# Attention scores by seven block products instead of eight, in a gated cross-attention and feed-forward block

## The chip, the cores and the metric

The kernel runs on one core of one Trainium2 chip. The metric is the device time of one execution in microseconds (us): 608.14 for the kernel before, the median of 3 runs (607.65 to 608.43). The engines are TensorE (PE; its weight loads are listed apart as PEld), VectorE (DVE), ScalarE (ACT), GpSimd (POOL) and SyncE (SP), which here issues every DMA. Each engine works through its own instructions in the order in which they are written; semaphores are all that ties them together.

## The reference

```
x   = x + tanh(g_xattn) * attn(layernorm(x), ctx, ctx, wq, wk, wv, wo)      # x: 4 x 512 x 512, ctx: 4 x 512 x 512
        q = xn wq^T;  k = [ctx, xn wk^T];  v = [ctx, xn wv^T]               # 512 queries, 1024 keys in each batch
        out = softmax(q k^T / sqrt(512)) v wo^T
x   = x + tanh(g_ffn) * ffn(layernorm(x))
        hidden = relu((xn sign(up)^T) * up_scale)                           # 2048 wide
        ffn = (hidden sign(down)^T) * down_scale * output_scale
```

All in float32. The four batches are independent.

## The kernel before, in words

**Precision.** TensorE is used at float32r. Each float32 operand is split in two, HI (ACT copies it to float32r) and LO (DVE or POOL subtracts HI from the original), and a product of split operands is three matmuls (`PASSES`, L14): HI·HI, HI·LO, LO·HI. A matmul here is always 128 x 128 weights against 512 columns.

**One batch of attention** on TensorE, in order: 96 matmuls of scores (4 tiles of 128 queries by two sides, "ctx" and "new", by 4 chunks by 3 passes), with the probabilities of each tile turned by 8 transposes through the two `turn` banks; 48 matmuls for V (`v_terms`, four jobs of 12); 96 for probabilities times V (`attn_terms`, four groups e = 0 to 3 of 24, each 12 "new" and 12 "old"); 48 for the output projection (`out_piece`); and 96 for the next batch's K and Q (eight jobs of 12). A job writes one PSUM bank; ACT takes HI from the bank, DVE then takes LO from the same bank, and only then is the bank free (`proj_out`, L754 and L994). Groups e = 0, 2 share bank 0 of `proj`, groups e = 1, 3 share bank 1.

**Scores and softmax** (L478, L1009, L758). A tile's 1024 scores stay in PSUM; DVE takes the maximum from there, ACT the exponential from there into `probs`, which has room for two tiles.

**Layernorm of the next batch.** DVE takes statistics of the next batch's rows (L1021, L1026, L1047), POOL the inverse deviation (L367). SP stores these facts to DRAM (`row_facts`, L306, 4 KB), waits for the store, and loads them back along the free axis for all partitions (`all_facts`, L309, 512 KB). DVE then normalises `turned_x`, the already transposed input (`norm_turned`, L1032 and L1035), ACT takes HI (L853), DVE takes LO (L1040), and K and Q of the next batch can start. In ACT's program L853 stands between the copies of groups e = 0 and e = 1. In DVE's program the statistics stand among the softmax of the batch, and `norm_turned` after V's last split.

**Context.** `raw_ctx` is loaded twice in a batch, transposed (for the scores) and plain (for the values). ACT splits off HI (L748), POOL takes LO (L382).

**Last batch.** Beside its attention the first rows of the feed-forward input are normalised, turned (`turn_two`) and copied out by ACT (L784), and the signs of the weights are taken by ACT (`take_signs`, L769 to L779) from one buffer `raw_w`, which SP refills (512 KB) after each (`load_signs`, L259). In ACT's program the first sign steps stand one behind each exponential. The feed-forward part (from about 374 us on) uses the same seven-product form that the change brings to the scores, and is not touched.

**Start.** ACT and POOL split the four weight matrices while TensorE makes K and Q of batch 0; ACT's program mixes these splits (`weight_high`, L744) with the copies of K and Q.

## Time and profile before

| | |
|---|---|
| time, median of 3 runs | 608.14 us (607.65 to 608.43) |
| the profiled execution's own time | 608.41 us |
| its span, first to last instruction | 606.6 us |
| TensorE busy | 598.5 us, 99% of the span |
| chain of work that ended last | 95% TensorE |
| granted TensorE clock, mean | 1.000 |
| a batch, from one batch's first score matmul to the next's | 90.7 us |

The profile is one execution. "Busy" of TensorE counts pipelined matmuls, so a row's mean time of one matmul (about 390 ns) is longer than the distance from one to the next; the distance is read from the starts of consecutive groups. Idle time of an engine stands in brackets, with what ended it. The program's lines (L454) are those of the kernel before.

### The profile page before, as it was taken

What the parts mean: (1) busy time and instruction counts of PE and PEld (TensorE: products, weight loads), DVE (VectorE), ACT (ScalarE), POOL (GpSimd) and SP (SyncE); (2) the same over time, 40 slices, a digit from 0 to 9 for tenths busy, and PEclk for the clock granted to TensorE, in tenths of its full rate; (3) what the DMA queues carried; (4) which work ended last, traced back from release to release, by engine and by line L of the source; (5) the groups of instructions that cost most, each with busy time, mean ns of one, the idle gap of its engine ahead of it and who ended that gap; (6) DMA issues with size and microseconds to landing.
All of it is one profiled execution on the core that took longest, in us unless ns stands there. A gap on an engine that the chain in (4) does not pass through costs nothing.

```text
span 606.6 us, 6935 instructions
## 1 busy us (share of the span) xinstructions
PE 598.5 (99%) x2786; PEld 496.8 (82%) x2786; DVE 298.5 (49%) x439; ACT 245.1 (40%) x366; POOL 126.5 (21%) x116
## 2 busy tenths in 40 slices
PE   8999999999999999999999999999999999999997
PEld 7888888888888888888888888888887878888885
DVE  4335532225632225632226658665548844766664
ACT  3723321213321214321125655564658545645531
POOL 5760303000303000303000305224132003242002
PEclk9999999999999999999999999999999999999999
DMA  8751303000303000503012212112121212241011
GB/s 299 273 171 38 106 1 110 29 0 1 104 1 131 8 0 1 239 4 104 1 36 70 89 52 78 62 35 71 35 70 35 83 56 70 70 133 42 1 70 69
DMA packets 20096, 43.20 MB, mean 71 GB/s; under 512 B 4832, under 2 KB 4832, under 8 KB 19680
## 3 DMA queue, kind: packets, MB, share of 16 engines
q1 hardware_dynamic: 20064, 42.76, 20.6%
q8 instruction: 22, 0.36, 0.3%
q14 instruction: 10, 0.08, 0.0%
HBM read 36.45 MB, written 6.30 MB: 70 GB/s over the span
## 4 chain that ended last, share of the span: by engine, by line
PE 95%; DVE 2%; ACT 1%; DMA 1%; SPq 0%; issue 0%; ACTq 0%
PE proj L454 33%; PE score L454 22%; PE score L532 19%; PE turn L517 12%; PE proj L517 5%; PE turn L446 2%; PE score L669 2%; DMA rows<-in_x 1%; PE proj L500 1%; PE turn L500 1%; DVE four_x L991 0%; ACT four_x L748 0%; DVE rows L1335 0%; DVE scaled L1332 0%; DVE neg_max L1011 0%; ACT probs L760 0%
## 5 line engine op out<-in xcount | busy, mean ns | idle before, releaser
L532 PE MATMUL score<-down_signs,hid_split 128*128 128x512 f32 x512 | 133.8, 390 | 0.6 <-DVE normed L1245 0.5
L532 PEld LDWEIGHTS score<-down_signs,hid_split 128*128 128x128 f32 x512 | 95.8, 188 | 21.7 <-DVE hid_split L1212 0.9
L756 ACT ACTIVATE four_x<-proj 128x512 fp32r<-128x512 f32 x60 | 35.8, 599 | 163.3 <-PE proj L454 163.3
L454 PE MATMUL score<-four_x 128*128 128x512 f32 x384 | 89.9, 391 | 0.0
L454 PE MATMUL proj<-probsT,four_x 128*128 128x512 f32 x384 | 88.4, 390 | 0.0
L454 PEld LDWEIGHTS proj<-probsT,four_x 128*128 128x128 f32 x384 | 71.9, 188 | 14.8
L454 PEld LDWEIGHTS score<-four_x 128*128 128x128 f32 x384 | 71.5, 188 | 14.5
L454 PE MATMUL proj<-four_x,weights 128*128 128x512 f32 x336 | 76.8, 389 | 0.0
L454 PEld LDWEIGHTS proj<-four_x,weights 128*128 128x128 f32 x336 | 63.0, 188 | 13.0
L997 DVE TENSOR_TENSOR four_x<-proj,four_x 128x512 fp32r<-128x512 f32 x44 | 30.3, 691 | 87.9 <-ACT four_x L756 87.9
L382 POOL TENSOR_TENSOR four_x<-raw_ctx,four_x 128x2048 fp32r<-128x2048 f32 x8 | 36.9, 4610 | 116.5 <-ACT four_x L748 116.5
L1212 DVE TENSOR_TENSOR hid_split<-hid,hid_split 128x512 fp32r<-128x512 f32 x64 | 44.0, 690 | 15.8 <-ACT hid_split L910 15.5
L517 PE MATMUL turn<-ops_b,up_ops 128*128 128x512 f32 x192 | 51.8, 391 | 0.0
L910 ACT ACTIVATE hid_split<-hid 128x512 fp32r<-128x512 f32 x64 | 39.9, 630 | 21.7 <-PE score L532 18.9
L760 ACT ACTIVATE probs<-score,neg_max 128x1024 f32<-128x1024 f32 x16 | 17.9, 1117 | 71.8 <-DVE neg_max L1011 71.8
L454 PE MATMUL proj<-weights,four_x 128*128 128x512 f32 x192 | 46.0, 394 | 0.3 <-DVE four_x L997 0.3
L454 PE MATMUL score<-weights,four_x 128*128 128x512 f32 x192 | 45.3, 389 | 0.0
L901 ACT ACTIVATE hid<-hid,hid_gain 128x512 f32<-128x512 f32 x48 | 34.8, 724 | 22.3 <-DVE hid L1227 11.0
L415 POOL TENSOR_TENSOR up_ops<-up_ops 128x256 fp32r<-128x256 f32 x16 | 13.3, 831 | 145.0 <-ACT up_ops L779 145.0
L454 PEld LDWEIGHTS score<-weights,four_x 128*128 128x128 f32 x192 | 36.0, 188 | 7.5
L517 PEld LDWEIGHTS turn<-ops_b,up_ops 128*128 128x128 f32 x192 | 35.7, 188 | 7.2
L454 PEld LDWEIGHTS proj<-weights,four_x 128*128 128x128 f32 x192 | 35.4, 188 | 7.5 <-DVE four_x L997 0.5
(102 smaller groups left out, 645.9 us busy)
## 6 DMA issues: line engine op xcount, KB each, us to landing
raw_w<-in_ffn_w SPq DMA_DIRECT2D x24, 512.0 KB, 3.3
raw_ctx<-in_ctx_turned SPq DMA_DIRECT2D x4, 1024.0 KB, 8.1
raw_ctx<-in_ctx SPq DMA_DIRECT2D x4, 1024.0 KB, 5.4
result<-rows SPq DMA_DIRECT2D x16, 256.0 KB, 2.1
rows<-in_x SPq DMA_DIRECT2D x3, 1024.0 KB, 5.5
turned_x<-in_x_turned SPq DMA_DIRECT2D x3, 1024.0 KB, 7.8
rows_away<-rows SPq DMA_DIRECT2D x1, 2048.0 KB, 10.4
rows<-rows_away SPq DMA_DIRECT2D x1, 2048.0 KB, 7.8
```

Of the source, the lines that this page charges most:

```text
L382: pool.tensor_tensor(ctx_side[:, LO], raw_ctx[:, :, :], ctx_side[:, HI].bitcast(F32), ALU.subtract).then_inc(ctx_ready, 1)
L415: pool.tensor_tensor(a[:, S3], a[:, A11].bitcast(F32), a[:, A21].bitcast(F32), ALU.subtract).then_inc(left_ready, 1)
L446: last = pe.transpose(bank[:, k * P:(k + 1) * P], tile, ident[:, :])
L454: last = pe.matmul(bank, lhs(l), rhs(r), start=start and i == 0, stop=stop and i == 2)
L517: last = pe.matmul(bank, up_ops[:, g % 2, left, c * P:(c + 1) * P], right(i)[:, s, c, :], start=start and c == 0 and s == HI, stop=stop an ...
L532: last = pe.matmul(wide(r), hid_split[:, n % HR, s, r * P:(r + 1) * P], down_signs[:, chunk_of(q), :], start=(q == 0 and s == HI), stop=(q ...
L756: act.activation(dst, proj_bank(n), ACT.Copy, scale=scale).then_inc(proj_hi, 1)
L760: act.activation(probs[:, t % 2, :], score[t % 2][:, :, :].rearrange("p a n -> p (a n)"), ACT.Exp, bias=neg_max[:, t:t + 1], accum_out=row ...
L901: act.activation(dst, src, ACT.Relu, scale=hid_gain[:, j:j + 1]).then_inc(relu_done, 1)
L910: act.activation(hid_split[:, n % HR, HI, :], src, ACT.Copy).then_inc(hid_hi, 1)
L997: dve.tensor_tensor(dst(LO), proj_bank(n), dst(HI).bitcast(F32), ALU.subtract).then_inc(proj_lo, 1)
L1212: dve.tensor_tensor(hid_split[:, n % HR, LO, :], src, hid_split[:, n % HR, HI, :].bitcast(F32), ALU.subtract).then_inc(hid_ready, 1)
```

## The change

The scores of a batch are taken as one product of a left matrix (Q, 512 x 512) and a right matrix (the keys, 512 x 1024), each cut in two by two blocks: A11, A12, A21, A22 on the left and B11, B21 (context) and B12, B22 (new keys) on the right. Seven block products of sums take the place of eight: S3·T3, S2·T2, S1·T1 and so on. Each is 2 tiles by 2 chunks by 3 passes, 12 matmuls, 84 in a batch. To form them, K and Q go from PSUM into SBUF unsplit (`raw_new`, `raw_q`), DVE makes the sums T1 to T4 and S1 to S4, ACT and DVE split each; after the products DVE adds PSUM banks and partial sums into `probs`, which now holds all four tiles in SBUF. Maximum and exponential work on `probs`.

The probabilities are turned in eight blocks of 4 transposes, one in the middle of each V job and one behind it. Before group e = 0 TensorE waits once for the splits of all four V jobs. `raw_ctx`, `turned_x` and `normed` are one memory. The statistics of the next batch, `norm_turned` and the sign steps stand at other places. Order of TensorE's products: A11, S3, A12, S2, S1, A22, S4.

```diff
-        probs = at("probs", 192, [P, 2, KEYS])
-        raw_ctx = at("raw_ctx", 200, [P, RT, DIM])
+        probs = at("probs", 192, [P, RT, KEYS])
+        first_normed = at("first_normed", 200, [P, RT, DIM])
+        raw_ctx = at("raw_ctx", 208, [P, RT, DIM])
         normed = at("normed", 208, [P, RT, DIM])
+        turned_x = at("turned_x", 208, [P, DC, ROWS])
+        raw_q = at("raw_q", 120, [P, DC, ROWS])
+        raw_new = at("raw_new", 152, [P, DC, ROWS])
+        raw_t = at("raw_t", 176, [P, KC, ROWS])
+        s3_op = at("s3_op", 216, [P, 2, 2, 2 * P], F32R)
...
+        SCORE_ORDER = (A11, S3, A12, S2, S1, A22, S4)
+        SCORE_RIGHT = {A11: B11, S3: T3, A12: B21, S2: T2, S1: T1, A22: T4, S4: B22}
+        TILE_ORDER = (2, 3, 0, 1)
+        OLD, NEW = 0, 1
+        TURN_ORDER = ((2, NEW), (2, OLD), (3, NEW), (3, OLD), (0, NEW), (1, NEW), (0, OLD), (1, OLD))
...
+            def context_rows(b):
+                sp.wait_ge(ctx_ready, turned_split(b) + 1)
+                sp.wait_ge(t_sums, nth(T_SUMS, b, T4))
+                sp.dma_start(raw_ctx[:, :, :], ctx_v[b]).then_inc(ctx_in, 16)
...
+                sp.wait_ge(ctx_ready, values_split(b - 1) + 1)
                 sp.dma_start(turned_x[:, :, :], x_turned_v[b]).then_inc(turned_x_in, 16)
                 sp.wait_ge(rstd_done, b)
                 sp.wait_ge(means_out, b)
                 sp.dma_start(row_facts[b - 1].rearrange("s r p -> p s r"), mean_rstd[:, :, :],
                              allow_slow_non_contiguous=True).then_inc(facts_stored, 16)
...
+                sp.wait_ge(scored, product_scored(b - 1, S3, 1))
                 sp.dma_start(all_facts[:, :, :], row_facts[b - 1:b].rearrange("a s r p -> a s (r p)").broadcast_to(
...
+            for b in range(BATCH):
+                context_rows(b)
+                if b + 1 < BATCH:
+                    next_rows(b + 1)
+                    sp.wait_ge(next_lo, b + 1)
+                    sp.dma_start(raw_ctx[:, :, :], ctx_turned_v[b + 1]).then_inc(ctx_in, 16)
...
             for i in range(DC):
                 weight_low(W_V, i)
             for b in range(BATCH):
+                context_low(values_split(b))
                 inverse_std(b + 1)
...
+            def score_product(b, i, t):
+                for c in range(2):
+                    for k, (l, r) in enumerate(PASSES):
+                        last = pe.matmul(score_bank(i, t), q_left(i, l)[:, c, t * P:(t + 1) * P],
+                                         key_right(SCORE_RIGHT[i], r)[:, c, :],
+                                         start=i in (A11, S3, S2) and c == 0 and k == 0, stop=c == 1 and k == 2,
+                                         skip_group_check=True)
...
+            def scores(b):
+                pe.wait_ge(ctx_ready, turned_split(b) + 1)
+                pe.wait_ge(s_ready, nth(S_LO, b, A11))
+                for t in range(2):
+                    pe.wait_ge(raw_kq, kq_out(b, DC + 2 + t))
+                    score_product(b, A11, t)
+                pe.wait_ge(t_ready, nth(T_LO, b, T3))
+                pe.wait_ge(s_ready, nth(S_LO, b, S3))
+                pe.wait_ge(attended, RT * b)
...
+                for r in range(RT):
+                    if r < 2:
+                        pe.wait_ge(score_c11, 2 * b + r + 1)
+                    else:
+                        pe.wait_ge(proj_lo, values_out(b, r - 2))
+                    for i, (lhs, rhs) in enumerate(v_terms(r)):
+                        last = product(proj_bank(proj0(b) + r), lhs, rhs, i == 0, i == DC - 1)
+                        if i == 1:
+                            turn_probs(b, 2 * r)
+                    last.then_inc(proj_done, 1)
+                    turn_probs(b, 2 * r + 1)
...
+                scores(b)
+                v_jobs(b)
+                pe.wait_ge(proj_lo, values_out(b, RT - 1))
+                pe.wait_ge(turn_lo, turn0(b) + 6)
                 for e in range(DC):
                     new, old = attn_terms(e)
-                    pe.wait_ge(proj_lo, n + 4 + e - 1)
+                    if e >= 1:
+                        pe.wait_ge(proj_lo, values_out(b, DC + e - 2))
                     for i, (lhs, rhs) in enumerate(new):
-                        if e == 0:
-                            pe.wait_ge(proj_lo, n + i + 1)
                         last = product(proj[:, e % 2, :], lhs, rhs, i == 0, False)
+                    if last_batch and e < 2:
+                        turn_two(RT * e)
                     if e == 0:
+                        pe.wait_ge(turn_lo, turn0(b) + 2 * RT)
...
+                n = e if b == 0 else proj0(b - 1) + 8 + e
+                act.wait_ge(proj_done, n + 1)
+                act.activation(raw_new[:, e, :], proj_bank(n), ACT.Copy).then_inc(raw_kq, 1)
...
+            def keys_and_queries(b, e):
+                if e < DC:
+                    key_out(b, e)
+                else:
+                    query_out(b, e - DC)
+                if e == 1:
+                    t_high(b, T1)
+                if e == DC:
+                    t_high(b, T3)
+                    t_high(b, T2)
+                if e == DC + 1:
+                    s_high(b, A11)
+                    s_high(b, S3)
+                    t_high(b, T4)
+                if e == DC + 2:
+                    t_high(b, B22)
...
                 context_high(values_split(b))
+                exponentials(b, 2)
...
+                proj_out(m + 3, new_side[:, HI, 3, :])
+                probs_out(b, 7)
                 if last_batch:
+                    for n in range(4):
+                        take_signs(n)
+                    two_rows_out(0)
                     take_signs(4)
...
+            def s_sum(b, i):
+                    dve.wait_ge(t_sums, nth(T_SUMS, b, T3))
+                    dve.wait_ge(raw_kq, kq_out(b, DC + 1))
+                elif i == S2:
+                    dve.wait_ge(raw_kq, kq_out(b, DC + 3))
+                    dve.wait_ge(s_ready, nth(S_LO, b, S3))
+                elif i == S4:
+                    dve.wait_ge(s_sums, nth(S_SUMS, b, S2))
+                dve.tensor_tensor(dst, one, two, op).then_inc(s_sums, 1)
...
+                bank = score[0 if k in (AT_P17, AT_C21) else 1][:, t, :]
+                if k in (AT_P17, AT_P16):
+                    plus = probs[:, t, 512:1024]
+                    dve.wait_ge(score_p1, 2 * b + t + 1)
+                else:
+                    plus = dst
+                    dve.wait_ge(score_sums, score_sum(b, {AT_C22: AT_P17, AT_C21: AT_P16, AT_C12: AT_P16}[k], t))
+                dve.wait_ge(scored, product_scored(b, last_product, t))
+                dve.tensor_tensor(dst, bank, plus, ALU.add).then_inc(score_sums, 1)
...
+            def keys(b):
+                t_sum(b, T1)
+                t_sum(b, T3)
+                t_sum(b, T2)
+                t_sum(b, T4)
+                t_low(b, T3)
...
+                proj_out(b, 3, chunk(new_side, 3))
+                probs_out(b, 7)
                 dve.wait_ge(exp_done, RT * b + RT)
...
+                    dve.wait_ge(ctx_ready, values_split(b) + 1)
+                    norm_rows(b + 1, 0)
+                    norm_stats(RT)
+                    norm_moments(BATCH + 1)
+                    proj_out(b, 4, chunk(qT, 0))
                     for f in range(RT, 2 * RT):
...
                 else:
-                    for e in range(DC):
-                        proj_out(m + 4 + e, chunk(qT, e))
-                        if e == 1:
-                            next_rows_low(b + 1)
+                    dve.wait_ge(x_in[b + 1], 16)
+                    norm_stats(next_tile0)
+                    norm_moments(b + 1)
+                    means(b + 1)
+                    proj_out(b, 4, chunk(qT, 0))
+                    norm_turned(b + 1)
+                    proj_out(b, 5, chunk(qT, 1))
+                    next_rows_low(b + 1)
+                    proj_out(b, 6, chunk(qT, 2))
+                    proj_out(b, 7, chunk(qT, 3))
+                if b + 2 == BATCH:
+                    norm_stats(0)
+                    norm_moments(BATCH)
+                keys(b + 1)
```

DVE, batch 0, from the first turned probabilities to the split of the next rows. L1021 to L1047 are the statistics of the next batch's rows, L1032 and L1035 its normalisation (`norm_turned`), L997 splits of V jobs and, behind L1129, of groups e. Before:

```order
L991 TENSOR_TENSOR probsT<-turn,probsT 128x4x128 x2
L1021 BN_STATS stats<-rows 128x6 x4
L1011 TENSOR_REDUCE neg_max<-score 128x1
L1026 BN_AGGR mean_var<-stats 128x2 x4
L1047 COPY mean_rstd<-mean_var 128x4
L991 TENSOR_TENSOR probsT<-turn,probsT 128x4x128 x2
L1011 TENSOR_REDUCE neg_max<-score 128x1
L991 TENSOR_TENSOR probsT<-turn,probsT 128x4x128 x2
L997 TENSOR_TENSOR four_x<-proj,four_x 128x512 x2
L991 TENSOR_TENSOR probsT<-turn,probsT 128x4x128 x2
L997 TENSOR_TENSOR four_x<-proj,four_x 128x512 x2
L1032 TENSOR_TENSOR turned_x<-turned_x,all_facts 128x2048
```

The same place after the change (L1179 is the split of V jobs and of groups e, L1174 of turned probabilities, L1288 to L1314 the statistics, L1299 and L1302 the normalisation, L1307 the LO part of the next rows):

```order
L1179 TENSOR_TENSOR four_x<-proj,four_x 128x512
L1174 TENSOR_TENSOR probsT<-turn,probsT 128x4x128
L1388 RECIPROCAL row_inv<-row_sum 128x4
L1392 TENSOR_SCALAR row_gain<-row_inv,gates 128x4
L1288 BN_STATS stats<-rows 128x6 x4
L1293 BN_AGGR mean_var<-stats 128x2 x4
L1314 COPY mean_rstd<-mean_var 128x4
L1179 TENSOR_TENSOR four_x<-proj,four_x 128x512
L1299 TENSOR_TENSOR turned_x<-turned_x,all_facts 128x2048
L1302 TENSOR_TENSOR turned_x<-turned_x,all_facts 128x2048
L1179 TENSOR_TENSOR four_x<-proj,four_x 128x512
L1307 TENSOR_TENSOR four_x<-turned_x,four_x 128x2048
```

The statistics moved from among the softmax, ahead of all V splits, to behind the last split of V and of the probabilities; the normalisation stands behind the split of group 0 and ahead of that of group 1.

ACT in the last batch, behind the last turned probabilities (L873) of that batch. L964 are sign steps, L969 copies of turned feed-forward rows, L877 the copy of group e = 0. After the change:

```order
L873 ACTIVATE probsT<-turn 128x4x128
L964 ACTIVATE down_signs<-raw_w 128x1024 x4
L969 ACTIVATE raw_x_72<-turn 128x4x128 x2
L964 ACTIVATE down_signs<-raw_w 128x1024
L877 ACTIVATE four_x<-proj 128x512
L969 ACTIVATE raw_x_72<-turn 128x4x128 x2
```

Before, the last of the sign steps that stand apart, with the same copies (L779 sign steps, L784 turned rows, L756 copies of V jobs 2 and 3):

```order
L779 ACTIVATE down_signs<-raw_w 128x1024
L756 ACTIVATE four_x<-proj 128x512
L784 ACTIVATE raw_x_67<-turn 128x4x128 x2
L756 ACTIVATE four_x<-proj 128x512
L784 ACTIVATE raw_x_67<-turn 128x4x128 x2
L779 ACTIVATE down_signs<-raw_w 128x1024
```

Four sign steps now follow one another without other work between them, and the copies that free the `turn` banks come behind them.

## Rows read from the trace of the kernel before

**Rows 1.** The page's busy table: engine, busy us (share of the span), instructions.
```profile
PE 598.5 (99%) x2786; PEld 496.8 (82%) x2786; DVE 298.5 (49%) x439; ACT 245.1 (40%) x366; POOL 126.5 (21%) x116
```

**Rows 2.** What TensorE waited for: us in total, times, longest.
```profile
PE score L676 <- DVE ones L1181: 1.2, 1, 1.2
...
PE proj L454 <- DVE four_x L997: 0.3, 1, 0.3
```

**Rows 3.** TensorE in order of time, batch 1: start us, us, instructions.
```profile
124.95 11.05 PE L454 MATMUL score<-four_x 128*128 128x512 f32 x48
135.84 1.03 PE L446 MATMUL turn<-ident,probs 128*128 128x128 f32 x8
136.63 5.71 PE L454 MATMUL score<-four_x 128*128 128x512 f32 x24
```

**Rows 4.** Timeline, a job's end, its two splits, and the next batch's statistics.
```profile
125.15 0.60 ACT L756 ACTIVATE four_x<-proj 128x512 fp32r<-128x512 f32 x1 [2.12 <-PE proj L454]
125.78 0.69 DVE L1000 SCALAR_TENSOR_TENSOR four_x<-proj,four_x 128x512 fp32r<-128x512 f32 x1 [2.03 <-ACT four_x L756]
...
143.73 0.37 DVE L1026 BATCH_NORM_AGGREGATE mean_var<-stats 128x2 f32<-128x6 f32 x4
...
145.50 0.37 SPq L306 DMA_DIRECT2D row_facts<-mean_rstd  x1
...
156.42 0.34 SPq L309 DMA_DIRECT2D all_facts<-row_facts  x1
...
162.67 2.28 DVE L1032 TENSOR_TENSOR turned_x<-turned_x,all_facts 128x2048 f32<-128x2048 f32 x1
164.98 2.29 DVE L1035 TENSOR_TENSOR turned_x<-turned_x,all_facts 128x2048 f32<-128x2048 f32 x1
...
167.36 1.91 ACT L853 ACTIVATE four_x<-turned_x 128x2048 fp32r<-128x2048 f32 x1
```

**Rows 5.** SP's two facts DMAs in the other batches, from its timeline.
```profile
54.83 0.37 SPq L306 DMA_DIRECT2D row_facts<-mean_rstd  x1
66.39 0.34 SPq L309 DMA_DIRECT2D all_facts<-row_facts  x1
...
236.18 0.37 SPq L306 DMA_DIRECT2D row_facts<-mean_rstd  x1
245.31 0.34 SPq L309 DMA_DIRECT2D all_facts<-row_facts  x1
```

**Rows 6.** The facts' load (line L309): issue to landing.
```profile
DMA to landing us min/median/max: 3.4/3.6/5.9
```

**Rows 7.** ACT and TensorE at the start.
```profile
20.68 0.60 ACT L756 ACTIVATE four_x<-score 128x512 fp32r<-128x512 f32 x1 [0.84 <-PE score L669]
21.18 1.14 ACT L744 ACTIVATE weights<-rows 128x512 fp32r<-128x512 f32 x2
...
23.36 11.07 PE L454 MATMUL proj<-four_x,weights 128*128 128x512 f32 x48
```

**Rows 8.** Groups of 1024 columns, and of the whole context: busy us, mean ns.
```profile
L1079 DVE TENSOR_TENSOR normed<-raw_x 128x1024 f32<-128x1024 f32 x2 | 2.4, 1217 | 0.0
...
L800 ACT ACTIVATE ops_a<-raw_x 128x1024 fp32r<-128x1024 f32 x8 | 8.3, 1055 | 0.0
...
L748 ACT ACTIVATE four_x<-raw_ctx 128x2048 fp32r<-128x2048 f32 x8 | 15.3, 1917 | 0.0
```

**Rows 9.** Last batch: two sign steps on ACT, and DVE around them.
```profile
345.46 0.17 DVE L1127 RECIPROCAL row_inv<-row_sum 128x4 f32<-128x4 f32 x1
...
345.80 1.91 DVE L1059 TENSOR_SCALAR normed<-rows,mean_var,mean_rstd 128x512 f32<-128x512 f32 x4
347.63 2.46 DVE L1021 BATCH_NORM_STATS2 stats<-rows 128x6 f32<-128x512 f32 x4
...
372.06 1.05 ACT L779 ACTIVATE down_signs<-raw_w 128x1024 fp32r<-128x1024 f32 x1
...
376.44 1.06 ACT L779 ACTIVATE up_ops<-raw_w 128x1024 fp32r<-128x1024 f32 x1 [0.78 <-DMA raw_w<-in_ffn_w]
```

**Rows 10.** TensorE, last batch: first score matmul, and the output projection's first.
```profile
306.31 11.05 PE L454 MATMUL score<-four_x 128*128 128x512 f32 x48
...
368.52 5.60 PE L454 MATMUL score<-weights,four_x 128*128 128x512 f32 x24
```

**Rows 11.** TensorE's first matmuls of 256 columns.
```profile
1.19 5.09 PE L676 MATMUL score<-ones 128*128 128x256 bf16 x23 [1.19 <-DVE ones L1181]
6.13 0.84 PE L446 MATMUL turn<-ident,normed 128*128 128x128 f32 x4
...
7.57 1.04 PE L676 MATMUL score<-ones 128*128 128x256 bf16 x8
```

More of the change, by code:

```diff
@@ L74, in sem @@
             return stack.enter_context(nc.semaphore(name))
+        A11, A12, A21, A22, S1, S2, S3, S4 = range(8)
+        B11, B21, B22, T1, T3, T2, T4 = range(7)
         KB = 1024
@@ L104, in gated_block @@
         hid1_slots = at("hid1", 112, [P, HC, ROWS])
-        A11, A12, A21, A22, S1, S2, S3, S4 = range(8)
         up_ops = at("up_ops", 144, [P, 2, 8, 2 * P], F32R)
@@ L491, in turn_probs, with score_bank @@
-            def turn_probs(b, t):
-                pe.wait_ge(exp_done, RT * b + t + 1)
-                for half in range(2):
-                    turn_job(turn0(b) + 2 * t + half, cols(probs[:, t % 2, half * 512:(half + 1) * 512]))
+            def score_bank(i, t):
+                if i in (A11, A12):
+                    return proj[:, t, :]
+                return score[0 if i in (S3, A22) else 1][:, t, :]
+            def score_product(b, i, t):
[5 more added lines that the diff above has]
+                                         skip_group_check=True)
+                last.then_inc(scored, 1)
@@ new lines, in first_products_out @@
+            def first_products_out(b):
+                s_high(b, A12)
+                s_high(b, S2)
+                for t in range(2):
+                    act.wait_ge(scored, product_scored(b, A11, t))
+                    act.activation(probs[:, t, 512:1024], proj[:, t, :], ACT.Copy).then_inc(score_p1, 1)
+                s_high(b, S4)
+                s_high(b, S1)
+                for t in range(2):
+                    act.wait_ge(scored, product_scored(b, A12, t))
+                    act.activation(probs[:, t, 0:512], proj[:, t, :], ACT.Copy).then_inc(score_c11, 1)
```

389 lines of the change are left out of this document (235 added, 154 removed).

## The prediction

> **What bounds the kernel now.** I read the busy table first: TensorE works 99% of the span, DVE 49%, ACT 40% [rows 1]. Then what TensorE waited for: nothing above 1.2 us, and in the attention 0.3 us [rows 2]. Then TensorE in order of time, where groups follow one another without a gap [rows 3]: 48 score matmuls from 124.95 to 135.84 are 0.227 us each; a block of 8 transposes takes 0.79 (135.84 to 136.63). So each matmul that goes is worth 0.227 us, and each wait that TensorE gets is paid in full. The other engines have idle time, but in fixed orders, so what counts is where their instructions stand.
>
> **Product count.** 96 score matmuls of a batch become 84: 12 x 0.227 = 2.7 us, over four batches **-10.9 us**. Eight blocks of 4 transposes for four of 8: at 0.79 for 8, no change.
>
> **Do the sums keep up?** Take t = 0 as the end of the last Q job. A job's end is followed by the copy after 0.20, the DVE step starts 0.63 after that and takes 0.69, 1.5 in all [rows 4]; DVE steps of 1024 columns take 1.22, ACT's 1.05 [rows 8]. T1 to T4 follow K's jobs, all summed by -6.3; the last raw Q copy ends at 0.8. A11 can start at 0 (tile 0 needs Q chunk 2 only) and S3 at 2.7 (its split ends near -2.5). A12 is due at 5.4, its split ends near 2.9; S2 due at 8.2, split near 3.6; S1 due at 10.9, split near 5.7; tile 1 of S1 at 12.2 needs the sum of S2's second bank, at 11.8, the narrowest place. The maximum of tile 2 ends near 17, that of tile 3 near 20; the first turned block is due at 20.4, the third at 24.0, when the first one's split ends near 23.3. So the score stage of a running batch costs nothing. If one link slips, a few tenths in each batch.
>
> **Start.** Here it does not keep up. ACT's program puts the new copies between weight splits. K's second copy ends at 21.3 [rows 7]. Then: T1 on DVE 1.2, its copy 1.05, weight pair 1.15, K2 0.6, context 1.9, K3 0.6, weight pair 1.15, Q0 0.6, which ends at 29.3 with ACT's overlaps. TensorE's Q jobs start at 23.36 [rows 7], and the third, due at 28.8, waits for that copy: 0.5. Two T copies, a weight pair and Q1's copy end at 32.9: fourth job 0.9. Then A11, S3, T4, a weight pair, Q2 end at 36.8 (1.2 lost at tile 0 of A11), B22, the last pair and Q3 at 39.5 (1.3 lost at tile 1). Sum **+4.0**, between 2 (T1 faster, overlaps larger) and 6.
>
> **V's last split.** Groups e took V's four splits one by one before. Now TensorE waits for all four before e = 0. The last V job's split is ready 1.5 after its end, and only one block of 4 transposes, 0.4, lies in between. 1.1 x 4 = **+4.5**. Between 1 and 1.5 each.
>
> **The facts of the next rows.** This is the main term. Before, DVE took the statistics among the softmax, so that the trip of the facts to DRAM and back lay beside V. Now they stand behind the last split. Let v be the end of the last V job. Split of V at v+1.5, of the last probabilities +2.2, reciprocal and gain 0.34 (+2.5) and four statistics 2.46 (+5.0) [rows 9], aggregates to the issue of the store 143.73 to 145.50, 1.8 (+6.8) [rows 4]. Store's issue to load's issue: 10.9 there, 11.6 and 9.1 in the other batches [rows 4, 5], mean 10.5 (+17.3). Load 3.6 (+20.9) [rows 6]. Two normalisation steps 162.67 to 167.27, 4.6 (+25.5); L853 on ACT 1.9 (+27.4) [rows 4]. Queued behind it on ACT is the copy of group e = 1, and behind the normalisation on DVE its split: 0.6 and 0.7 (+28.7). That split frees bank 1 of `proj`, for which group e = 3 waits. TensorE has groups 0, 1, 2 as cover: 1.5 + 72 x 0.227 = +17.8. So it waits 10.9 us in batches 0, 1 and 2: **+32.7**. With the shortest trip (9.1 + 3.4) 9.3 each, with the longest (11.6 + 5.9) 14.3. Behind that nothing else is late: K and Q need the next rows' LO part (2.3 us of DVE more), and TensorE has e = 3 and the output projection, 72 x 0.227 = 16 us, before them. POOL's inverse deviation and the load of `turned_x` stand behind the context's split, which ends some 18 us ahead of v.
> The Trainium skill (DMA: Bandwidth & Descriptors, Anatomy of one DMA) gives about 2.0 us of fixed cost for a DMA of its GpSimd path. Taken for the 4 KB store the wait would be about 8.5 shorter in each batch, an estimate by that page; the trace shows 9.1 to 11.6 three times, so I go by the trace.
>
> **Signs in the last batch.** ACT takes four sign steps in a row. `raw_w` is one buffer, so each waits for its refill: from one start to the next 372.06 to 376.44, 4.4 us [rows 9]. After the last turned probabilities at v+1.4: first sign until +2.5, the fourth until +15.6, and only then the copy of the first turned feed-forward row, +16.2, for which the third block of turns waits. TensorE is there at 1.5 + 2.7 + 0.8 + 2.7 = +7.8: 8.4 us. Then the fifth sign (+20.0), the copy and split of e = 0 (+21.3), and behind it on DVE the next normalised row (0.5, +21.8), due at +19.8: 2.0. Together 10.4. From the batch's first score to the output projection it took 62.2 before [rows 10], of which 240 x 0.227 + 8 x 0.79 = 60.8 is work: 1.4 of old waits go. **+9.0**, between 5 and 13.
>
> **TensorE's clock.** TensorE's first 23 matmuls of 256 columns, after it had done nothing, took 4.9 us, 0.215 each, and 8 like them at 7.57 took 1.04 with the last one's tail [rows 11]. 256 columns in 0.215 us is the lower level, 1.2 GHz, though the view gives 1.000 as the mean granted clock. An idle stretch of 10.9 us may do the same again: half of 4.9 is 2.5 us lost behind each of the three waits. In the last batch most of it falls into the second wait, 0.5. **+8.0**, between 0 (no fall) and 12.
> The Trainium skill (TensorE: Matmul & The Clock Gate, The HAM clock gate) says that the clock is halved after an idle stretch and comes back after sustained work. By that the drop comes at each of the long waits; the rows of before agree for the start, and hold no long wait later that could test it.
>
> **Sum**, on the profiled execution's own 608.4: -10.9 + 4.0 + 4.5 + 32.7 + 9.0 + 8.0 = +47.3, so 655.7. The median of the runs is 0.3 below that execution. I say **656 us**.
>
> **Rivals.**
> The clock stays up through waits of 10 us. For it: in all rows the granted clock reads 1.000. Against it: the start's matmuls. 656 - 8 = 648 us.
> The facts return early, since in the new order no other transfer is in flight. For it: the range 9.1 to 11.6 within one run. Against it: at 145.50 to 156.42 nothing else was in flight either, and it took 10.9. With a trip of 6 instead of 14.1 the wait is 2.8 each and the clock has no reason to fall: 656 - 24.3 - 7.5 = 624 us.
> More waits than I counted, at the joints of the score stage (0.4 of slack at S1) or with a longer slow stretch of the clock behind each wait: 1 us in each batch and 4.9 for the 2.5 of each fall give 656 + 4 + 7 = 667 us.
> Faster than before: the cover holds everywhere and only the product count is left. This is one mechanism, the facts' trip: it decides from where the split of e = 1 is ready at v+17.8, which needs a trip of 3.2 us instead of 14.1. Then, if also the sign steps found cover, 608.4 - 10.9 + 4.0 + 4.5 = 606; with no wait at the start or behind V either 597.5. Against it stand the three measured trips.
>
> **How the numbers follow.** The forecast (640 to 661 on its own) 0.55, the steady clock 0.17, the early facts 0.10, more waits 0.13, faster 0.05. The range goes from 642, below the steady clock's case with the shortest trip in part, to 666, near the third rival: what is left out is the early facts, the faster case and the outer part of the others, about 0.2. What a measurement can tell from no change here is about 0.2%, 1.2 us: faster by more 0.04, within 0.01, slower 0.95.
>
> **What would show it.** In the profile after: 336 score matmuls; TensorE idle about 11 us before group e = 3 in batches 0, 1, 2, put down to the split of e = 1 (DVE) with the facts' load ahead of it; about 1 us before e = 0 in each batch; 8 and 2 us among the turned rows of the last batch, ended by ACT or DVE behind the sign steps; about 4 us over the last Q jobs and A11 of batch 0; and matmuls at twice the distance, with a granted clock below 1, behind each long wait. The period of a batch goes from 90.7 to 90.7 - 2.7 + 1.1 + 10.9 + 2.5 = 102.5 us. A period of 88 to 90 would prove the main term wrong, as would facts that are stored before the last split of V.

## The result, and the profile after

The changed kernel takes 663.73 us (median, 663.20 to 664.76) against 608.08 for the kernel before on the same chip: a ratio of 1.092, 95% interval 1.090 to 1.094. The profiled execution has a span of 662.5 us where before it was 606.6, so 55.9 us are to be found. In each fence below the lines are those of the kernel named ahead of it.

The changed kernel's page, its busy table, and what TensorE waited for (us in total, times, longest), to be read against [rows 1, 2]:

```profile
PE 602.3 (91%) x2738; PEld 494.3 (75%) x2738; DVE 382.2 (58%) x527; ACT 290.0 (44%) x426; POOL 132.7 (20%) x116
```

```profile
PE proj L527 <- DVE four_x L1179: 35.2, 7, 11.2
PE turn L625 <- ACT raw_x L969: 7.7, 1, 7.7
PE proj L527 <- ACT raw_q L888: 5.8, 2, 5.6
PE proj L560 <- ACT raw_q L888: 1.9, 1, 1.9
```

There are 48 matmuls fewer, as the product count says, and yet TensorE is busy 3.8 us longer: it is slower somewhere. And there are now four kinds of wait where there was hardly any.

**Start.** TensorE in order of time, changed kernel, from Q's four jobs (the first two on one line) over the first score product (A11, at 44.99) to the second (S3, at 49.61):

```profile
23.96 5.63 PE L527 MATMUL proj<-four_x,weights 128*128 128x512 f32 x24
29.79 3.01 PE L527 MATMUL proj<-four_x,weights 128*128 128x512 f32 x12 [0.19 <-ACT raw_q L888]
38.37 4.75 PE L527 MATMUL proj<-four_x,weights 128*128 128x512 f32 x12 [5.58 <-ACT raw_q L888]
44.99 4.78 PE L560 MATMUL proj<-four_x 128*128 128x512 f32 x12 [1.87 <-ACT raw_q L888]
49.61 2.89 PE L560 MATMUL score<-probsT,s_op 128*128 128x512 f32 x12
```

A product of 12 matmuls takes 2.72 from its start to the next one's, so a score stage at full speed that reaches S3 at 49.61 would have begun at 46.89. Before, it began at 34.27. The start costs 12.6 us. In it are the two waits of 5.6 and 1.9, the two groups that took 4.8 us where 12 matmuls take 2.9, and a first Q job 0.6 later than in [rows 7]. The slow groups are the clock's: it read 0.72 around the first of them and 0.66 around the second (45.00 to 50.00). The first stretch (start and end us, length, busy us of PE, PEld, DVE, ACT, POOL, the granted clock, DMA share, GB/s):

```profile
38.40:45.00 6.60, 4.73 (x13) 3.48 (x13) 6.50 (x6) 3.74 (x7) 3.84 (x3) 0.72 0.00 0
```

DVE and POOL in the same stretch:

```profile
21.99 1.23 DVE L1200 TENSOR_TENSOR raw_t<-raw_new,raw_ctx 128x1024 f32<-128x1024 f32 x1 [3.93 <-ACT raw_new L883]
28.15 5.25 DVE L1200 TENSOR_TENSOR raw_t<-raw_new 128x1024 f32<-128x1024 f32 x1 [4.93 <-ACT raw_new L883]
33.32 2.29 DVE L1200 TENSOR_TENSOR raw_t<-raw_new,raw_t 128x1024 f32<-128x1024 f32 x1
35.65 2.18 DVE L1200 TENSOR_TENSOR raw_t<-raw_ctx,raw_t 128x1024 f32<-128x1024 f32 x1
```

```profile
27.71 4.60 POOL L455 TENSOR_TENSOR four_x<-raw_ctx,four_x 128x2048 fp32r<-128x2048 f32 x1 [0.26 <-ACT four_x L869]
32.27 4.46 POOL L450 TENSOR_TENSOR weights<-probs,weights 128x512 fp32r<-128x512 f32 x2
```

The four lines of DVE are the same instruction at the same size: T1, T3, T2, T4. T1, with nothing of POOL beside it, takes 1.23. T3 begins 0.44 behind POOL's context split and ends 1.1 behind that split's end (28.15 + 5.25 = 33.40, 27.71 + 4.60 = 32.31), as if it did nothing until POOL was through and then took its own time; experiments 3 and 4 test this. Each of POOL's two W_O splits behind it takes 2.23, where 1.3 is usual.

**A batch.** SP, DVE and ACT of the changed kernel, from the statistics behind batch 0's last split of probabilities to the split for which group e = 3 waits (the answer to [rows 4]):

```profile
83.16 2.47 DVE L1288 BATCH_NORM_STATS2 stats<-rows 128x6 f32<-128x512 f32 x4
...
102.34 2.29 DVE L1299 TENSOR_TENSOR turned_x<-turned_x,all_facts 128x2048 f32<-128x2048 f32 x1 [12.88 <-DMA all_facts<-row_facts]
104.66 2.29 DVE L1302 TENSOR_TENSOR turned_x<-turned_x,all_facts 128x2048 f32<-128x2048 f32 x1
109.41 0.69 DVE L1179 TENSOR_TENSOR four_x<-proj,four_x 128x512 fp32r<-128x512 f32 x1 [2.46 <-ACT four_x L877]
```

```profile
87.45 0.37 SPq L379 DMA_DIRECT2D row_facts<-mean_rstd  x1
98.49 0.34 SPq L384 DMA_DIRECT2D all_facts<-row_facts  x1
```

```profile
106.99 1.91 ACT L1044 ACTIVATE four_x<-turned_x 128x2048 fp32r<-128x2048 f32 x1 [18.25 <-DVE turned_x L1302]
```

TensorE beside it, and a stretch with the granted clock (columns as above):

```profile
82.37 16.61 PE L527 MATMUL proj<-probsT,four_x 128*128 128x512 f32 x72 [0.98 <-DVE four_x L1179]
110.16 7.45 PE L527 MATMUL proj<-probsT,four_x 128*128 128x512 f32 x24 [11.18 <-DVE four_x L1179]
117.44 0.84 PE L527 MATMUL score<-weights,four_x 128*128 128x512 f32 x3
```

```profile
110.00:114.00 4.00, 3.84 (x9) 3.05 (x10) 2.90 (x3) 0.00 (x0) 0.00 (x0) 0.52 0.05 18
```

The chain is the one of the forecast: statistics behind the last split, a store that needs 11.0 to the load's issue, two normalisation steps, ACT's copy, the late split of e = 1. The wait ahead of e = 0 is 1.0. Behind the wait of 11.2 the granted clock is 0.52 for 4 us, the lower of TensorE's two levels, and e = 3 takes 7.28 from its start to the next group's, not 5.44. In batches 1 and 2 the wait is 10.4 and 9.8, the group 7.58 and 8.08. From one batch's first score product to the next's it takes 102.0 and 101.9 (150.08, 252.09, 353.98), and 103.2 from the 46.89 worked out above to 150.08. Before, it was 90.7.

**Last batch.** TensorE of the changed kernel around its wait:

```profile
392.40 2.98 PE L527 MATMUL proj<-probsT,four_x 128*128 128x512 f32 x12
403.05 1.97 PE L625 MATMUL turn<-ident,normed 128*128 128x128 f32 x8 [7.67 <-ACT raw_x L969]
404.67 4.27 PE L527 MATMUL proj<-probsT,four_x 128*128 128x512 f32 x12
```

ACT ahead of it, changed kernel (the copy for which TensorE waits is the third line):

```profile
397.12 1.06 ACT L964 ACTIVATE down_signs<-raw_w 128x1024 fp32r<-128x1024 f32 x1 [3.34 <-DMA raw_w<-in_ffn_w]
401.45 1.06 ACT L964 ACTIVATE down_signs<-raw_w 128x1024 fp32r<-128x1024 f32 x1 [3.27 <-DMA raw_w<-in_ffn_w]
402.41 1.06 ACT L969 ACTIVATE raw_x<-turn 128x512 f32<-128x512 f32 x2
```

Sign steps 4.3 to 4.4 apart, as in [rows 9]. From the first score product (353.98) to the output projection (424.32) it is 70.3 us, 8.1 more than [rows 10]. The feed-forward network behind it takes 238 us in both kernels.

The 55.9 us are thus 12.6 at the start, 35.0 in the three periods, 8.1 in the last batch, and 0.2 for rounding and the feed-forward part.

### The profile page after: what moved, and what is told of

It is laid out like the page before. It is cut to its first block, busy times and chain, and to the rows that moved or that the text cites. A ratio compares the mean times of both kernels' runs of the same rounds, so it can differ in the third digit from the quotient of the medians.

```text
span 662.5 us, 7100 instructions
## 1 busy us (share of the span) xinstructions
PE 602.3 (91%) x2738; PEld 494.3 (75%) x2738; DVE 382.2 (58%) x527; ACT 290.0 (44%) x426; POOL 132.7 (20%) x116
## 4 chain that ended last, share of the span: by engine, by line
PE 68%; DMA 9%; issue 8%; DVE 8%; ACT 5%; POOL 2%; SPq 0%; POOLq 0%; DVEq 0%; ACTq 0%
PE proj L527 19%; PE score L657 17%; PE turn L642 11%; PE score L527 7%; DMA row_facts<-mean_rstd 4%; PE proj L642 4%; PE score L560 4%; PE proj L560 2%; DMA all_facts<-row_facts 2%; DVE raw_t L1200 2%; DMA raw_w<-in_ffn_w 1%; POOL four_x L455 1%; PE score L788 1%; DVE turned_x L1299 1%; DVE turned_x L1302 1%
## 5 line engine op out<-in xcount | busy, mean ns | idle before, releaser
L527 PE MATMUL proj<-probsT,four_x 128*128 128x512 f32 x384 | 97.7, 416 | 35.2 <-DVE four_x L1179 35.2
L527 PEld LDWEIGHTS proj<-probsT,four_x 128*128 128x128 f32 x384 | 76.8, 203 | 53.9 <-DVE four_x L1179 37.5
L527 PE MATMUL proj<-four_x,weights 128*128 128x512 f32 x336 | 79.2, 396 | 5.8 <-ACT raw_q L888 5.8
L1179 DVE TENSOR_TENSOR four_x<-proj,four_x 128x512 fp32r<-128x512 f32 x32 | 22.0, 689 | 54.4 <-ACT four_x L877 54.4
L527 PE MATMUL proj<-weights,four_x 128*128 128x512 f32 x192 | 51.9, 405 | 0.0
L877 ACT ACTIVATE four_x<-proj 128x512 fp32r<-128x512 f32 x32 | 18.7, 593 | 55.9 <-PE proj L527 55.9
L527 PEld LDWEIGHTS proj<-weights,four_x 128*128 128x128 f32 x192 | 34.0, 189 | 5.9
L642 PE MATMUL proj<-ops_a,up_ops 128*128 128x512 f32 x128 | 34.6, 392 | 0.0
L1243 DVE TENSOR_TENSOR probs<-score,probs 128x512 f32<-128x512 f32 x40 | 27.5, 689 | 11.6 <-PE score L560 11.2
L642 PE MATMUL turn<-ops_a,up_ops 128*128 128x512 f32 x128 | 34.2, 389 | 0.0
```

Of the source, the lines that this page charges most:

```text
L527: last = pe.matmul(bank, lhs(l), rhs(r), start=start and i == 0, stop=stop and i == 2)
L642: last = pe.matmul(bank, up_ops[:, g % 2, left, c * P:(c + 1) * P], right(i)[:, s, c, :], start=start and c == 0 and s == HI, stop=stop an ...
L877: act.activation(dst, proj_bank(n), ACT.Copy).then_inc(proj_hi, 1)
L1179: dve.tensor_tensor(dst(LO), proj_bank(proj0(b) + i), dst(HI).bitcast(F32), ALU.subtract).then_inc(proj_lo, 1)
L1243: dve.tensor_tensor(dst, bank, plus, ALU.add).then_inc(score_sums, 1)
```

## The experiments

All runs are compared with the kernel before on their own chip; its median was 607.96 to 608.59. Names are those of the changed kernel's program.

**1. Statistics two batches ahead.**

```
 # DVE, batch(b), between V's splits and proj_out(b, 4)
-    dve.wait_ge(x_in[b + 1], 16)
-    norm_stats(next_tile0); norm_moments(b + 1); means(b + 1)
 # DVE, behind attend(b, r), ahead of keys(b + 1)
+    dve.wait_ge(x_in[b + 2], 16)
+    norm_stats(RT * (b + 2)); norm_moments(b + 2); means(b + 2)      # b = 0 and 1
 # and those of batch 1 between T1 and T3 of batch 0
```

> The changed kernel with one edit: the statistics of the rows two batches on are taken on DVE behind the output projection's last additions (those of batch 1 between T1 and T3 of batch 0), so that the facts are stored from about 17 us after a batch's first score product on instead of 7 us behind the last V job. Theory (the facts' trip is late, and its idle stretch drops TensorE's clock): the waits before group e = 3 in batches 0 to 2 (11.5, 10.7 and 10.1 us by the starts of the groups) and the slow matmuls behind them (1.8, 2.1, 2.6 us) go: 663.7 - 32.3 - 6.6 = 625 us. Rival (the split of e = 1 is late for another reason in ACT's or DVE's order): the waits stay, 663 us. Rival (the clock falls for another reason): the waits go and e = 3 still takes 7.3 to 8.1 us instead of 5.4: 631 us.

Measured: 625.08 us (624.75 to 626.16), ratio 1.027 (1.025 to 1.030): 38.65 us less. TensorE, batch 0 of this kernel: all four groups e in one stretch.

```profile
81.59 22.05 PE L527 MATMUL proj<-probsT,four_x 128*128 128x512 f32 x96 [0.98 <-DVE four_x L1179]
```

The three waits ahead of e = 3 (11.18, 10.39 and 9.78, by the starts 32.2 in all) and the slow groups behind them (6.6) are 38.8. The main term and the clock's term behind its waits have their cause shown.

**2. The last batch's sign steps spread among the score copies and probabilities.**

```
 # ACT, last batch
     context_high(values_split(b))
+    take_signs(0); take_signs(1)
     ...
     probs_out(b, 3)
+    take_signs(2)
     ...
     probs_out(b, 5)
+    take_signs(3)
     ...
-    for n in range(4): take_signs(n)
     two_rows_out(0)
```

> The changed kernel with one edit: in the last batch the first four sign steps stand apart in ACT's program, two ahead of the first exponential, one each behind the turned blocks 3 and 5. Theory (a row of sign steps waits for the refills of one buffer, and the copy that frees the turn bank stands behind it): the wait of 7.7 us before the third pair of turned rows goes, and the 1 to 2 us behind it: 663.7 - 10 = 654 us. Rival (the turned rows wait for something else, normalised rows or POOL): the wait stays, 663 us.

Measured: 653.00 us (652.00 to 656.94), ratio 1.074 (1.070 to 1.078): 10.7 us less. TensorE of this kernel goes through the same place without a wait:

```profile
391.56 2.99 PE L527 MATMUL proj<-probsT,four_x 128*128 128x512 f32 x12
394.39 1.04 PE L625 MATMUL turn<-ident,normed 128*128 128x128 f32 x8
```

**3 and 4. What stretched the T sums?** One kernel holds POOL's context split and W_O splits back until T4 is summed, the other holds back only a load of 1 MB that runs in the same stretch.

```
 # 3: POOL
+    pool.wait_ge(t_sums, nth(T_SUMS, 0, T4))
     context_low(turned_split(0))
 # 4: SP
+    sp.wait_ge(t_sums, nth(T_SUMS, 0, T4))
     sp.dma_start(rows[:, 2 * RT:3 * RT, :], x_v[2]).then_inc(x_in[2], 16)
```

> The changed kernel with one edit: at the start POOL waits for T4's sum before it splits the context, so that POOL does nothing while DVE takes T3, T2 and T4. Theory A (DVE steps with two SBUF operands and POOL's two-operand steps shut each other out): T3's sum takes 1.2 us instead of 5.25, T2's and T4's 1.2 instead of 2.3 and 2.2; Q's second raw copy comes about 5 us earlier, the fourth Q job no longer waits 5.6 us, the clock stays up there; POOL's context split then runs against T3's split and the S sums, which gives a part back: 663.7 - 3 to - 7, about 659 us. Theory B (the load of 1 MB of rows that lands in those 5 us slows DVE): T3 stays at 5.25, and the time does not fall.

> The changed kernel with one edit: at the start the load of batch 2's rows (1 MB, issued at 27.5 us) waits for T4's sum, so that no transfer lands while DVE takes T3, T2 and T4; POOL works as in the changed kernel. Theory A (POOL and DVE shut each other out): T3's sum stays at 5.2 us and the time is the same, 663.7. Theory B (the transfer slows DVE): T3's sum takes 1.2 us and the time falls by about 8, to 656.

Measured: 664.64 us (662.82 to 666.86) and 664.67 us (663.52 to 664.91), both ratio 1.092. With the load held back T3 still took 5.26: the transfer is not the cause. With POOL held back, DVE of that kernel, T3, T2, T4, the split of T3, and then S3's sum, which takes 0.68 by itself:

```profile
26.95 1.23 DVE L1201 TENSOR_TENSOR raw_t<-raw_new 128x1024 f32<-128x1024 f32 x1 [4.94 <-ACT raw_new L884]
28.09 1.22 DVE L1201 TENSOR_TENSOR raw_t<-raw_new,raw_t 128x1024 f32<-128x1024 f32 x1
29.35 1.23 DVE L1201 TENSOR_TENSOR raw_t<-raw_ctx,raw_t 128x1024 f32<-128x1024 f32 x1
30.49 1.22 DVE L1206 TENSOR_TENSOR probsT<-raw_t,probsT 128x1024 fp32r<-128x1024 f32 x1
32.03 4.66 DVE L1223 TENSOR_TENSOR raw_new<-raw_q 128x512 f32<-128x512 f32 x1 [0.32 <-ACT raw_q L889]
```

```profile
30.65 5.49 POOL L455 TENSOR_TENSOR four_x<-raw_ctx,four_x 128x2048 fp32r<-128x2048 f32 x1 [4.40 <-DVE raw_t L1201]
```

The mechanism is shown in both directions: each engine's step gets longer when it comes second. POOL's split, which came while DVE worked on the split of T3, takes 5.49 instead of 4.6; DVE's sum, which came while POOL worked, ends 0.55 behind POOL's end. But the time did not fall: the fourth Q job now waits 0.5 instead of 5.6, while A11 waits 4.9 and A12 2.6. I had expected 659. The stall was moved onto the next steps of DVE, since POOL's work still lay among them.

This kernel's cost is one of pairing. In the kernel before, POOL does the same context and W_O splits at the start (4.63, and 5.05 for four) and DVE's steps beside them read one operand from PSUM and take 0.69 each, unchanged. The change brings steps of DVE with both operands in SBUF, and these are the ones that stretch. The Trainium skill (SBUF — State Buffer, SBUF: two separate sides) states this: of a DVE instruction with two SBUF inputs and a GpSimd instruction that reads SBUF, the one that starts first keeps their common port pair for its whole length, and "the other fully blocks". By that rule T3 costs the 4.2 that were left of POOL's split and its own 1.2, together 5.4; the trace has 5.25 and agrees.

**5. TensorE kept at work in the gap.**

```
 # TensorE, V's group e = 3 of batches 0 to 2, ahead of its wait
+    for _ in range(88):
+        pe.matmul(turn[:, 0, 0:2 * P], ones[:, 0:P], ones[:, :], start=True, stop=True)
```

> The changed kernel with 88 matmuls of 256 columns added in front of TensorE's wait for the facts of rows (before V's group e=3) in batches 0, 1 and 2: they write to the PSUM tile turn, whose contents nobody reads then, and nobody waits for them. They fill what is idle in the changed kernel (waits of 11.2, 10.4 and 9.8 us in its trace; 88 x 0.107 us at the full clock is 9.4 us). Theory, that the slow group e=3 (7.28, 7.58, 8.08 us against 5.44) is a granted clock that falls because TensorE stands idle ahead of it: with the work in the gap, the clock stays up, e=3 takes 5.4 to 5.5 us in each batch, and the time falls by 6.6 us, to 657. Rival, that e=3 is slow for another reason (its operands, or what the other engines do beside it): e=3 stays at 7.3 to 8.1 us, the time stays at 664. Rival 2, that the fillers come too late or last too long: at 0.107 us each they end before the facts come, if the clock is at half when they run they take 0.21 us each and add up to 8 us per batch, to 680.

Measured: 656.99 us (655.84 to 657.79), ratio 1.079 (1.077 to 1.081): 6.7 less. TensorE of this kernel, batch 0, and its granted clock:

```profile
97.30 9.78 PE L734 MATMUL turn<-ones 128*128 128x256 bf16 x88
108.26 5.75 PE L527 MATMUL proj<-probsT,four_x 128*128 128x512 f32 x24 [1.18 <-DVE four_x L1182]
```

```profile
110.00:114.00 4.00, 4.00 (x19) 3.33 (x18) 1.01 (x2) 0.00 (x0) 0.00 (x0) 1.00 0.53 184
```

More work, less time: e = 3 waits for the same split and then takes 5.59 from its start to the next group's instead of 7.28, at a granted clock of 1.00 instead of 0.52. The slow groups e = 3 come from the idle time ahead of them.

**6 and 7. V's splits one by one, alone and with 1 and 2.**

```
 # TensorE, ahead of group e = 0
-    pe.wait_ge(proj_lo, values_out(b, RT - 1))
 # inside group e = 0, ahead of product i
+    pe.wait_ge(proj_lo, values_out(b, max(i, 2)))
```

> The changed kernel with TensorE's group e=0 waiting for V's splits one by one (the last only ahead of its products with r=3), as the kernel before does. Theory A, that in the changed kernel other chains set the end of this stage (the facts of rows in batches 0 to 2, the signs in the last): e=0 to e=2 begin 1.0 to 1.2 us earlier and the wait ahead of e=3 grows by as much (11.2 to 12.3 us); the time stays at 664 within 1 us. Theory B, that the wait for the last split adds itself, as the forecast's sum had it (4.5 us for four batches): 659.

> Three edits at once: statistics of rows two batches ahead (e1_facts_early), the last batch's sign steps spread among the score products (e2_signs_spread), and V's splits waited for one by one (e6_v_one_by_one). If the costs add: 663.7 - 38.6 (measured by the first) - 10.7 (by the second) - 4.5 (four times the 1.1 us wait for V's last split, which now is on the path) = 610. Then what is left over the kernel before (608) is the later score stage of batch 0 (12.6 us) less what the twelve fewer matmuls in each batch give (10.9). Rival, that the first two share a cost or that another chain takes over: 615 to 620, with a wait of over 1 us left in V's stage of batches 0 to 2.

Measured: alone 663.17 us (662.03 to 664.04), ratio 1.090 (1.088 to 1.092), which cannot be told from the changed kernel: the waits ahead of e = 0 are gone (3.9 in all), those ahead of e = 3 are 2.2 longer in all, and the one ahead of the turned rows is 1.2 longer. Together 610.59 us (610.09 to 611.08), ratio 1.003 (1.002 to 1.004). From 663.73 the first two edits take 49.4, each measured alone, and leave 614.35 if they add, so the third is worth 3.8 us here; the first two without the third were not run. The same edit gives nothing while a longer chain ends the stage, and its price once that chain is gone.

**8. The start in another order.**

```
 # DVE splits the first context itself, ahead of T1
+    dve.wait_ge(ctx_hi, 1)
+    dve.tensor_tensor(ctx_side[:, LO], raw_ctx[:, :, :], ctx_side[:, HI].bitcast(F32), ALU.subtract)
     keys(0)
 # POOL
-    context_low(turned_split(0))
+    pool.wait_ge(s_ready, nth(S_LO, 0, S3))
     for i in range(DC): weight_low(W_O, i)
 # ACT: context_high first, W_V's splits behind the copies of A12's product
 # DVE: batch 1's statistics among V's splits of batch 0
```

> The three edits of e7_three_mended, and another order at the start: the context is split before X's products need VectorE (its high half by ScalarE, its low half by VectorE), W_O's low halves by GpSimd come behind S3's split, W_V's splits and the fourth batch's load of rows behind the first score factors, and batch 1's statistics stand inside V's stage. So no GpSimd step lies beside VectorE's sums T3, T2, T4 and S3. Theory, that the later score stage (12.6 us in the changed kernel) comes from VectorE's sums and GpSimd's splits that shut one another out: the sums take 1.2 us each and the score stage begins 3 to 5 us later than before; 610 - 9 = 601, under the kernel before. Rival, that the chain of six sums and six splits on two engines costs as much by itself, or that what was moved is late in its new place (context or W_O's split ahead of V's groups): no less than 606, with waits of over 3 us in V's stage or before A11.

Measured: 609.32 us (607.30 to 612.62), ratio 1.002 (1.000 to 1.003). A miss of 8 us: the rival of the expectation (no less than 606, with waits at V's stage) came true, and the trace says where. TensorE of this kernel, and its granted clock behind the first wait:

```profile
42.53 4.58 PE L563 MATMUL proj<-four_x 128*128 128x512 f32 x12 [2.23 <-DVE four_x L1245]
...
92.98 8.21 PE L530 MATMUL proj<-probsT,four_x 128*128 128x512 f32 x24 [3.96 <-DVE four_x L1197]
```

```profile
42.00:47.00 5.00, 4.47 (x13) 3.56 (x14) 4.91 (x8) 2.06 (x3) 0.00 (x0) 0.66 0.00 0
```

A11 now goes at 34.70, without a wait. But POOL's four W_O splits (34.10 to 41.93) now lie beside S2, S4 and A12's split, 1.75 each instead of 0.68, and the facts of batch 1 are late again (3.96, and 2.6 in a slow e = 3). The edit did not keep all of DVE's sums clear either: POOL's four W_Q splits (19.45 to 28.07) lie beside T3 and T2, which take 2.28 and 2.32, but here TensorE waits for neither.

**9. Again, with these two mended.**

```
 # POOL
-    for i in range(DC): weight_low(W_O, i)
 # DVE takes them between T2's split and S1's sum, one or two at a time
+    out_weight_low(b, 0) ... out_weight_low(b, 3)
 # DVE: batch 1's statistics into the gaps ahead of the sums of C22, C21
```

> e8_start_too with two more edits. The statistics of batch 1's rows go from V's stage into the gaps of VectorE's score sums of batch 0 (about 15 us earlier), since in e8_start_too the facts came too late once more: TensorE waited 4.0 us ahead of e=3 in batch 0 and ran 24 matmuls there in 8.21 us instead of 5.44. And VectorE, not GpSimd, takes W_O's low halves, since GpSimd's stood beside VectorE's S2, S4 and A12 steps (1.75 us each instead of 0.68) and TensorE waited 2.2 us for A12 and ran its block product in 4.58 us instead of 2.88. Theory: both waits and both slow stretches go, 6.8 + 3.9 us, and the time is 609.3 - 10.7 = 599, with scores of batch 0 at one 2.88 us after another from A11 on. Rival A, that VectorE with four more steps (2.7 us alone) is late for A12 or S2: 602 to 604. Rival B, that the clock is slow after A11 for another reason than the wait ahead of it: 601.

Measured: 602.68 us (600.90 to 603.37), ratio 0.991 (0.990 to 0.993): faster than both kernels, 5.3 us under the one before. It falls in the expected band of rival A. Two things were changed at once, but each can be read at its own wait: A12 follows at once (below), and batch 0's four groups e run in one stretch again (96 matmuls in 22.03). DVE in this kernel, W_O's split, S2's sum, W_O's split, S4's sum:

```profile
35.67 0.69 DVE L1287 TENSOR_TENSOR weights<-probs,weights 128x512 fp32r<-128x512 f32 x1
36.27 0.69 DVE L1238 TENSOR_TENSOR raw_new<-raw_q,raw_new 128x512 f32<-128x512 f32 x1
36.88 0.69 DVE L1287 TENSOR_TENSOR weights<-probs,weights 128x512 fp32r<-128x512 f32 x1
37.48 0.69 DVE L1238 TENSOR_TENSOR raw_new<-raw_q,raw_new 128x512 f32<-128x512 f32 x1
```

TensorE in the same kernel goes from one product to the next until 45.0, and then waits once:

```profile
39.60 2.88 PE L561 MATMUL proj<-four_x 128*128 128x512 f32 x12
42.32 2.88 PE L561 MATMUL score<-probsT,four_x 128*128 128x512 f32 x12
47.99 5.96 PE L561 MATMUL score<-probsT,four_x 128*128 128x512 f32 x24 [2.79 <-DVE probs L1259]
```

With POOL empty, DVE does more and is in time: A12 needs no wait, and the granted clock of 34 to 42 is 1.00. The 2.8 that is left stands ahead of S1, for which VectorE is late. POOL's W_V splits now begin at 44.55, and the split of B22 beside them, at 44.95, takes 2.30 instead of 1.22, ahead of the sum (47.17 to 47.85) that TensorE waits for. That is 1.1 of the 2.8; DVE has no gap from 42.0 to that sum, so the rest lies in the number of its steps, W_O's four (2.8) among them. This is rival A's mechanism one product later than it was expected. Neither part was tried by itself. The profiled execution is also the fastest of the four, 1.8 under their median; its mean granted clock was 1.000, that of the others 0.996 and 0.993.

## Why the prediction was right, and where it was not

The forecast was 656 us, 642 to 666; measured 663.7. The direction, the main term and the range held. The order of the terms did not: the start, forecast as the smallest cost, came second. And the range held with some luck: 663.7 lies outside the forecast's own band of 640 to 661 and nearer to the third rival's 667, for which the range had been drawn up to 666. By its own terms, in us:

| term | forecast | measured | by |
|---|---|---|---|
| product count | -10.9 | -10.9 | 48 matmuls fewer, 0.227 apart |
| start | +4.0 | +12.6 | S3 at 49.61; experiments 3, 8, 9 |
| V's last split | +4.5 | +4.9 | four waits of 0.97 or 0.98, by the starts 1.2 each; 3.8 by experiment 7 |
| facts of rows | +32.7 | +32.2 | three waits; experiment 1 |
| signs, last batch | +9.0 | +9.6 | 8.1 + 2.7 - 1.2 (V's wait), with the slow clock there; experiment 2: 10.7 |
| clock | +8.0 | +6.6 | three groups e = 3; experiment 5: 6.7 |

The measured column sums to 55.0 of the 55.9; 0.7 of the rest is the score stage of batch 0 (19.7 instead of 19.0, with a wait of 0.4 at 58.35).

- *The facts of the next rows.* Right in mechanism, place and size (10.9 each forecast; 11.5, 10.7, 10.1 by the starts). Taking the trip from the trace was right: from the store's issue to the load's it was 11.0, 10.4 and 8.4, against a forecast of 10.5, and the period of a batch was 102.0 and 101.9, against 102.5. The rival of early facts is dead, and with it that of a faster kernel. That of more waits (667) came nearer in time than the forecast, but not by its mechanism: its waits at the joints of the score stage did not come in the running batches, and its longer slow stretches did not either.
- *The clock.* Right behind the long waits: the steady-clock rival (648) is refuted by the granted clock of 0.52 and by experiment 5. Half the start's 4.9 us was a fair price, 1.8 to 2.6 being measured. The part that it missed is that waits of 5.6 us or less at the start also cost it: those slow groups (4.75 and 4.78) sit in the term "start".
- *Signs.* The first wait was forecast at 8.4 and is 7.7; the second, of 2.0, did not come by itself. In its place TensorE worked slowly (4.27 for a group of 12, 1.97 for a block) until the next copies were there.
- *V's last split.* The size was right as a wait of TensorE (1.1 each forecast, 1.2 by the starts). That it adds is true only beside the other chains' removal (experiments 6, 7).
- *Start.* This is the term that was mis-sized: +4.0, "between 2 [...] and 6", measured 12.6; the 8.6 between them are more than the whole miss of 7.7. The step that failed is "T1 on DVE 1.2" carried on to all sums of DVE. The laid-out chain is good up to the copy of the first Q job, which was to end at 29.3 and ends at 29.6. The second's was to end at 32.9 and ends at 38.2, since it stands in ACT's program behind the copies of T3 and T2, whose sums DVE ended at 33.4 and 35.6. I laid ACT's program out step by step and took DVE's and POOL's durations from places where they were not beside each other. The trace of before had the warning, and I took the row of the undisturbed steps [rows 8]. Its DVE and POOL in the feed-forward network's start, where both have their operands in SBUF:

```profile
368.12 1.77 DVE L1079 TENSOR_TENSOR raw_x<-raw_x 128x1024 f32<-128x1024 f32 x1
```

```profile
367.20 1.60 POOL L415 TENSOR_TENSOR up_ops<-up_ops 128x256 fp32r<-128x256 f32 x1 [15.32 <-ACT up_ops L779]
```

  The same DVE step takes 1.22 elsewhere, and POOL's takes 0.83. The mean of that row's group (1.33 for five) says little of it; its maximum (1.77, with a median of 1.22) shows it.
- *Do the sums keep up?* In running batches, yes: 84 matmuls in 19.0 us, and the next wait is the one ahead of e = 0.

## What to carry to other kernels

When a change gives VectorE steps with both operands in SBUF, lay GpSimd's program beside them before pricing them: a step costs what is left of GpSimd's instruction plus itself, and giving the work to VectorE can be cheaper than sharing (experiment 9), as long as VectorE has the time. Price an edit by the chain that ends last at its place: here 1 us per batch was worth nothing until the two longer chains, that of the facts and that of the signs, were gone. And count each long wait of TensorE twice, for the idle time and for the slow matmuls behind it.

## What the runs showed of the hardware

- VectorE and GpSimd, both with two operands in SBUF: 1.23 us became 5.25, 0.68 became 4.66, and GpSimd's 4.6 became 5.5. With alternating short steps 1.22 became 2.2 to 2.3, 0.68 became 1.75, and GpSimd's 1.3 became 2.2. Steps with one operand in PSUM kept their 0.69.
- The granted clock fell to its lower level in waits of 9.8 to 11.2 us, and TensorE lost 1.8, 2.1 and 2.6 us until it was back. In the wait of 11.2 (98.98 to 110.16) it read 1.00 up to 102 and 0.50 from 104 on. Around a wait of 2.2 us (experiment 8, 40.3 to 42.5) it read 1.00 in the wait and 0.50 from 44 to 47, so it fell behind the wait, with TensorE at work again, and that product took 4.58 instead of 2.88. At the changed kernel's start it fell twice: 0.50 from 36.5 to 40, in and behind the wait of 5.6, 1.00 from 43.2 to 45, the wait of 1.9, and 0.50 again from 46 to 48. Around one of 2.8 (experiment 9, 45.2 to 48.0) it read 1.00 throughout. So the length of the last wait alone does not tell; what does was not tried.
- 88 needless matmuls of 256 columns in each of three batches made the kernel 6.7 us faster.
- A store of 4 KB took 11.0, 10.4 and 8.4 us from its issue to its landing in the changed kernel, 13.0 in batch 0 of experiment 1, where a load of 1 MB had been issued 1.3 ahead of it; the load of 512 KB behind the store took 3.7 to 5.1. Little of the store's time is transfer: of the 15 us from 87 to 102, in 40 slices, the DMA engines are busy in three (88.1 to 89.2) with the store, then in none up to the load, which is issued at 98.49. What the 9 us between are spent on no view shows.

```profile
DMA  0002720000000000000000000000000005999220
```
